# Reordering the line reloads, the rows of maxima and GpSimd's masks in the first batch of an attention and expert layer

## What is computed

```
scores = einsum('bhtd,bhsd->bhts', q, k) * scale      # causal, softmax over s
seq_out = softmax(scores) @ v
w1, w2 = x_prev @ w1w.T, x @ w2w.T ; r1, r2 = x @ r1w.T, x @ r2w.T     # 4 numbers a head
write_lines, read_lines = exterior(w1, w2), exterior(r1, r2)           # 6 products of pairs, normalised
M_all[t] = decayed sum over s < t of outer(Jw[s], Jw[s])               # 6 x 6 a head
mem_score = (1-alpha) * rd.M.rd + alpha * |rd.M|^2
gated = mean over heads of sigmoid(mem_score * mem_scale) * gate
x = layernorm(x + (seq_out + gated * mem_val) @ out_w.T + out_b)
x = layernorm(x + top-2-of-10 mixture of 8 expert matrices (x))
```

## Time and profile before

| | us |
|---|---|
| median of three runs | 825.11 |
| span of the profiled execution | 832.4 |
| PE busy | 734.4 (88%) |
| DVE busy | 603.8 (73%) |
| POOL busy | 422.3 (51%) |
| ACT busy | 351.0 (42%) |

### The profile page before, as it was taken

The page is one execution under the profiler, slowest core; times in us unless marked ns, Lnnn a source line. Parts: engine busy times, 40 slices in busy tenths (PEclk is TensorE's granted clock), DMA queues, the critical chain, the costliest instruction groups (busy, mean ns, idle before and its releaser), DMA issues.

```text
span 832.4 us, 12395 instructions
## 1 busy us (share of the span) xinstructions
PE 734.4 (88%) x4004; PEld 495.0 (59%) x4004; DVE 603.8 (73%) x2105; ACT 351.0 (42%) x701; POOL 422.3 (51%) x334
## 2 busy tenths in 40 slices
PE   6993998898898998999898998878899899998995
PEld 3452655565565666565565664446677676776774
DVE  2344776778878888889688877736777877787785
ACT  2211555446454545555455555842242242232410
POOL 9200894996665676668476893424134042240410
PEclk9995999999998999999899997899999999999998
DMA  7899589675564574655734747220220302303000
GB/s 274 257 234 165 127 142 144 163 115 104 130 102 84 133 119 100 152 85 138 139 69 105 139 87 170 73 101 2 77 85 18 101 10 93 102 1 102 26 24 27
DMA packets 60420, 89.88 MB, mean 108 GB/s; under 512 B 8234, under 2 KB 37316, under 8 KB 60356
## 3 DMA queue, kind: packets, MB, share of 16 engines
q1 hardware_dynamic: 60356, 89.09, 47.7%
HBM read 54.72 MB, written 33.82 MB: 106 GB/s over the span
## 4 chain that ended last, share of the span: by engine, by line
PE 47%; DVE 23%; DMA 10%; POOL 9%; ACT 4%; issue 4%; SPq 2%; ACTq 0%; POOLq 0%; DVEq 0%
PE ps L1256 15%; PE ps L374 8%; PE ps L338 7%; PE ps L327 6%; PE ps L315 6%; DVE ps L468 5%; DMA Wm<-mem_scratch 3%; DVE Ob L516 3%; DMA Q<-MT 3%; DVE A L1390 3%; ACT X L1242 2%; PE ps L1221 2%; PE ps L232 1%; POOL Pr L612 1%; DVE Z L1276 1%
## 5 line engine op out<-in xcount | busy, mean ns | idle before, releaser
L468 DVE CUSTOM_DVE_ANT_0 ps<-ps,mask 128x256 f32<-128x256 f32 (+3 forms) x512 | 236.9, 509 | 31.8 <-PE ps L315 31.0
L411 ACT ACTIVATE Pr<-ps 128x512 f32<-128x512 f32 (+2 forms) x384 | 190.1, 528 | 114.8 <-PE ps L327 110.6
L327 PE MATMUL ps<-Q,K 98*128 98x256 f32 (+2 forms) x512 | 173.2, 380 | 28.9 <-DMA Q<-MT 21.9
L315 PE MATMUL ps<-K,Q 96*128 96x256 f32 (+2 forms) x512 | 157.9, 355 | 23.2 <-DVE nmax L468 22.5
L1256 PE MATMUL ps<-ew_hi,XT 128*128 128x512 f32 x512 | 176.2, 403 | 0.0
L1390 DVE SCALAR_TENSOR_TENSOR A<-ps,cw,A 128x256 f32<-128x256 f32 x256 | 123.6, 483 | 48.5 <-PE ps L1256 36.0
L327 PEld LDWEIGHTS ps<-Q,K 98*128 98x128 f32 x512 | 94.1, 197 | 104.8 <-ACT Pr L411 61.0
L612 POOL TENSOR_SCALAR_AFFINE_SELECT Pr<-Pr 128x512 f32<-128x512 f32 x128 | 88.3, 704 | 103.2 <-ACT Pr L411 100.8
L315 PEld LDWEIGHTS ps<-K,Q 96*128 96x128 f32 x512 | 103.0, 203 | 45.8 <-DVE nmax L468 28.3
L1256 PEld LDWEIGHTS ps<-ew_hi,XT 128*128 128x128 f32 x512 | 97.0, 189 | 21.2 <-issue 0.3
L1256 PE MATMUL ps<-ew_rest,XT 128*128 128x512 f32 x256 | 101.2, 395 | 0.0
(11 more groups left out here) (190 smaller groups left out, 1049.2 us busy)
## 6 DMA issues: line engine op xcount, KB each, us to landing
qk_scratch<-HL SPq DMA_DIRECT2D x32, 512.0 KB, 3.2
Q<-qk_scratch SPq DMA_DIRECT2D x96, 128.0 KB, 4.4
K<-qk_scratch SPq DMA_DIRECT2D x96, 128.0 KB, 5.7
Pr<-xT SPq DMA_DIRECT2D x8, 512.0 KB, 7.0
xraw<-xT SPq DMA_DIRECT2D x8, 512.0 KB, 6.4
mem_scratch<-Rl SPq DMA_DIRECT2D x16, 256.0 KB, 7.5
mv_scratch<-MV SPq DMA_DIRECT2D x32, 128.0 KB, 1.8
Wm<-mem_scratch SPq DMA_DIRECT2D x16, 256.0 KB, 9.3
```

The lines of the kernel that those rows point to most:

```text
L315: last = nc.tensor.matmul(o, Q[0:STACK, hh, P * i:P * i + P], K[0:STACK, hh, 0:n], start=True, stop=True)
L327: last = nc.tensor.matmul(o, K[0:STACK + 2, hh, P * kt:P * kt + P], Q[0:STACK + 2, hh, T - n:T], start=True, stop=True)
L411: nc.scalar.activation(probs(g % 2, kt, heads[0], len(heads)), src, ACT.Exp, scale=SCALE).then_inc(s_exp, 1)
L468: last = nc.vector.tensor_tensor_reduce(out=scores, in0=scores, in1=mask[:, T - w:T], scale=1.0, scalar=NEG, op0=ALU.add, op1=ALU.max, acc ...
```

## The change

Three edits. SP sends group 0's rows of maxima first, then all 8 DMAs of the first reload (with all waits on the stores ahead of them, not half). The second reload is one piece of 8 DMAs, asked for at the fourth group (g = 3) ahead of that group's projected part and of the rows of maxima for batch 1's first group. GpSimd masks all of group 0 before it waits for the first reload, and its later masks move up by one group's worth between the lines.

```diff
@@ sp_batch
+                if first and g == NG - 1:
+                    sp.wait_ge(s_ml, ML_WRITE)
+                    read_rows()
                 if not last:
                     sp_projected(sp, b + 1, 2 * g)
                 if not (last and g == NG - 1):
                     sp_max_rows(sp, b + (g + 1) // NG, (g + 1) % NG)
-                if first and g >= 2:
-                    sp.wait_ge(s_ml, ML_WRITE)
-                    read_rows(g - 2)
@@ block.sync
-            for i in range(6):
-                sp.wait_ge(s_p1st[i], 16 * ((NB - i + 5) // 6))
-            mem_rows(0, 0, 8, Wm, range(4))
             sp_max_rows(sp, 0, 0)
             for i in range(6):
                 sp.wait_ge(s_p1st[i], 16 * ((2 * NB - i + 5) // 6))
             sp.wait_ge(s_gst, NB * 16)
-            mem_rows(0, 0, 8, Wm, range(4, NB))
-            sp_batch(sp, 0, first=True, read_rows=lambda h: mem_rows(1, 8, 8, Wm, range(4 * h, 4 * h + 4)))
+            mem_rows(0, 0, 8, Wm)
+            sp_batch(sp, 0, first=True, read_rows=lambda: mem_rows(1, 8, 8, Wm))
@@ block.gpsimd
+            m0, m1, m2, m3 = (group_masks(0, g) for g in range(NG))
+            masks(*m0)
             pool.wait_ge(s_mw[0], NB * 16)
-            m0, m1, m2, m3 = (group_masks(0, g) for g in range(NG))
-            lines(Jl, 0, 4, 1, lambda q: q, (1, 4), (m0[0:2], m0[2:4], [], m1[0:2], m1[2:4], []))
+            lines(Jl, 0, 4, 1, lambda q: q, (1, 4), (m1[0:1], m1[1:2], m1[2:4], [], m2[0:2], m2[2:4]))
-            norms(Jl, Rl[:], Ob[:, 2, :], (m2[0:3], m2[3:4]))
+            norms(Jl, Rl[:], Ob[:, 2, :], (m3[0:2], m3[2:4]))
-            masks(*m3)
```

## The result

The changed kernel takes 841.57 us (median of 4 runs, 839.74 to 845.48), against 826.65 us for the kernel before (4 runs): a ratio of 1.0189, 95% interval 1.0152 to 1.0225, so **14.9 us slower** by the medians. When both were run again later, the changed kernel gave 843.54 against 829.72, ratio 1.0140 (1.0105 to 1.0174). Runs over 1.5% above the fastest of the same kernel on the same chip count as slow and are left out of the ratios; with them left out, the means of all runs (9 of the changed kernel, 74 of the kernel before) differ by 13.0 us. The profiled execution took 840.0 us, of them 838.3 in the span.

The account below looks back on a forecast made before the run. PE, busy for 734 of 832 us, bounds the kernel, waiting on small DMAs behind loads. 14.7 + 2.5 - 1.7 = +15.5, rounded to +15, on the median of 825.1 gives 840 us; range 829 to 846 (8 in 10).

Parts of the forecast that it names:

- The likeliest case: For the whole kernel: the forecast outcome, slower at 836 to 845 us; chance 0.64.
- The clock: PE at half clock behind its long waits: 3.3 us lost in group 1, +2.5 us behind the wait at batch 1.
- rival (d): At SP's wait for the lines: SP is held, `ML_WRITE` after 125, time 845 us or more; chance 0.06.
- The large term: Second reload in one piece, ahead of batch 1's rows: PE idles 14 us, +14.7 us in all at this point.
- (a): At group 1 of batch 0: the early gain of 7.3 us survives, giving 817.8 us; chance 0.06.
- (b): At batch 1's start: its rows don't wait for all eight loads, giving 827 us; chance 0.12.
- (c): In batches 1 to 5: half is given back later, giving 831 to 834 us; chance 0.12.
- the sign that I had named for being wrong: The shift at 150 us is there but the span hasn't grown by it, so later stages give it back.
- My +15: Total loss by batch 1: 14.7 + 2.5 - 1.7 = +15.5 us, rounded to +15; bounds +11 to +19.

Follow-up runs that it names:

- Half the bytes: Changed kernel with each DMA of the second reload cut to 128 KB from 256 KB: 835.23 against 829.72 us for the kernel before, ratio 1.0068.
- the first of the two versions: Changed kernel with first reload split around group 0's rows, second reload split four and four, masks six blocks ahead: 846.95 against 828.2 us, ratio 1.0226.
- edit 3 alone: Kernel before with only the second reload made one piece, asked for at the fourth group: 842.0 against 829.32 us, ratio 1.0154.
- edits 2 and 3: Kernel before with the earlier masks and the one-piece second reload, without the early rows: 843.2 against 829.72 us, ratio 1.0159.
- edit 2 alone: Kernel before with only GpSimd's masks of group 0 ahead of the first reload's wait, later masks moved up: 835.61 against 829.32 us, ratio 1.0074.
- edit 1 alone: Kernel before with only group 0's rows sent first, then all eight DMAs of the first reload: 833.02 against 828.2 us, ratio 1.0033.

## Why the prediction was right, and where its terms were off

The forecast was 840.0, slower. The likeliest case came, by its mechanism. Step by step, in us (after: first profile of the changed kernel, with the second in brackets):

| step | predicted | after |
|---|---|---|
| PE starts attention | 71 | 68.7 (69.4) |
| group 1 starts; wait ahead of it | 92.5; 7.7 | 90.7; 8.69 (92.5; 9.79) |
| half clock behind it | 7.5 | 5.8 |
| group 2 starts | 108.7 | 106.1 (107.3) |
| stack of group 2 issued; landed | 122.0; 130.4 | 119.3; 128.0 |
| eight loads | 16.9 | 18.4 |
| batch 1 starts; wait ahead of it | 148.9; 14 | 147.2; 14.94 (147.5; 14.01) |
| half clock behind it | 9.1 | 4.0 |
| batch 1's group 1 starts | about 166 | 162.5 (163.0) |

**Edit 1.** The place was right: the gain is gone one group later. The size was off by 2 us. I let the gate rows' stores land at 70.33, as before; with no load among them they landed at 68.3. Everything up to the stack is earlier by about as much, and at group 2 only 0.2 us are lost where I had 2.8. In the second pair of profiles it is 107.3 against 107.8; counted from the turning of group 0's maxima (L358 at 61.69 and 63.44 before, 61.34 and 62.15 in the changed kernel), the two pairs lose 0.6 and 0.8.

**The clock.** This term was too large at both places: 5.8 us at half clock instead of 7.5 behind the wait of 8.69, and 4.0 instead of 9.1 behind the longest wait. I had carried over the 9.1 us of the earlier trace rows as if a longer idle time meant a longer recovery. That step failed. The 3.5 us that I took as the base were no fixed term either: in the second profile of the kernel before, PE runs on at full clock behind the wait of 0.99 us. What I charged for each us at half clock does come out: group 1 lasts 15.4 us in the changed kernel, and 13.8 + 5.8 x 0.44 - 0.88 is 15.4. Group 0 of batch 1 lasts 15.3 us, not the 17 between the starts that the sum implies.

**Edit 2.** It costs nothing in the changed kernel, as predicted: the first line product starts at 92.10 (predicted 93.4), the lines are done at 120.2 (predicted 122 to 124), and SP asks at 122.05. The margin is 1.9 us. Alone, against the kernel before, the same edit costs 6 us, through the wait that my rival (d) named, at the group where that kernel asks. GpSimd's timeline of the changed kernel (the last mask of group 0, the first product, the last product of the write lines, the first of the read lines):

```profile
91.49 0.64 POOL L612 TENSOR_SCALAR_AFFINE_SELECT Pr<-Pr 128x512 f32<-128x512 f32 x1 [10.21 <-ACT Pr L411]
92.10 1.09 POOL L798 TENSOR_TENSOR Ob<-Wm 128x511 f32<-128x511 f32 x1
...
118.88 1.28 POOL L801 TENSOR_TENSOR Jl<-Ob 128x511 f32<-128x511 f32 x1
...
146.59 1.27 POOL L798 TENSOR_TENSOR Ob<-Wm 128x512 f32<-128x512 f32 x1 [8.38 <-DMA Wm<-mem_scratch]
```

**Edit 3.** The large term was right in place and size: 2.3 us for each load instead of 2.1 (18.4 for the eight, 1.5 more), and the stack 2.4 us earlier, which nearly cancel. Half the bytes take 10 of the 15 us of wait away, and the edit alone costs 12.7 us. The wait of 0.84 for a mask is gone, as predicted.

**The cause behind it.** I had written that what stands in SP's queue ahead of the rows decides. For all loads on that queue the count comes out right, but the run with ScalarE's queue shows that loads in another queue hold them as well. A remedy drawn from my sentence (another queue) would have failed, and did.

**Rivals.** (a), the early gain survives, has the wait of 8.69 against it; a kernel in which it does survive to group 1 (the first of the two versions) loses it elsewhere. (b), the rows get past the loads, has 19.80 us against it. (c), half is given back later: from the start of batch 1's group 1 to that of the last group of attention it is 383.6 and 381.7 us in the two profiles of the kernel before, and 377.2 and 380.7 in those of the changed one. The first of these is 6 us shorter, which the second pair does not repeat. So the spans of the first pair differ by only 5.9 us (838.3 less 832.4), where the shift at batch 1's group 1 is 12.1: the sign that I had named for being wrong, in that pair. In the second pair the spans differ by 11.2 (842.1 less 830.9). Between the starts of batch 1's group 2 and of the last group, the windows of the kernel before and of the changed one are:

```profile
166.50:534.00 367.50, 334.78 (x2023) 212.17 (x2021) 299.08 (x1074) 196.62 (x396) 242.03 (x161) 0.94 0.57 116
```

```profile
178.00:539.70 361.70, 328.99 (x2021) 209.51 (x2022) 296.92 (x1068) 196.66 (x397) 239.89 (x158) 0.96 0.58 118
```

The granted clock was 0.94 in one execution and 0.96 in the other. With edit 3 alone (380.6), the reload on ScalarE's queue (380.9), and edits 2 and 3 (385.2), all of which reach this stretch 8.8 to 11.7 us late, it isn't systematically shorter than with edit 2 alone (378.7), edit 1 alone (381.5) or half the bytes (385.1). Over all runs the times differ by 13.0 us, a little more than the shift of 12.1. So nothing that these runs can show is given back; a microsecond or two stays open.

**The sum.** The profiles have a shift of 12.1 us at batch 1's group 1 (162.5 less 150.4; 163.0 less 150.8 in the second pair gives 12.2), or 12.5 and 13.4 if each is counted from the turning of group 0's maxima, and the times of all runs together 13.0. My +15 was about 2 too large, by the clock term and the early 2 us. That the first comparison gave 14.9 and that the forecast of 840 lies only 1.6 us from its median of 841.57 is partly luck: the shift was 2 us too large, and the median that the forecast started from, 825.11, is 3.8 below the mean of the kernel before over all its runs, 828.9.

## What to carry to other kernels

Before moving a small transfer that PE waits for, count the transfers in flight ahead of it on all queues and multiply by the trace's own time for each; a bulk load in one piece must be shorter than the work that covers it, wherever it is put. An early start is worth only what the next transfer on which the same engine waits lets through. And an edit that costs nothing in one order of the list can cost 6 us in another, so price each wait at the place at which it is asked for.

## What the runs showed of the hardware that I had not expected

- A transfer of 8 KB took 15.7 us to land though the eight loads of 256 KB issued ahead of it were on the other engine's queue. For 8 us (132 to 140) no packet of its own queue ran. With all on one queue it took 19.8, in the kernel before 10.8.
- After 14.94 us of idle time PE ran 4.0 us at half the granted clock, after 8.69 us 5.8, after 10.46 us 9.1; in the second profiles 4.6 after 9.79 and 9.3 after 10.60. In these five the recovery did not get longer with the idle time.
- A single execution of the same kernel lies within some 10 us of the median (819.1 to 836.0 us around 829.4 in 70 runs), and its mean granted clock (0.941 to 0.966) goes with most of that.
